# A graph kernel on one core: the node table stored twice, masked by mate, and 192 fetches of the search for 256

## The reference, cut to what matters

```python
h = (x_flat @ W_gat).reshape(M, HEADS, NUM_EXPERTS)      # 16 numbers a node
a_src = (h * att_src).sum(-1); a_dst = (h * att_dst).sum(-1)   # 4 scores each
e = leaky_relu(a_src[src] + a_dst[dst], 0.2)
alpha = softmax of e over the edges of one target node (a self loop is among them)
agg = segment_sum(h[src] * alpha[:, :, None], dst) + b_gat
scores = layernorm(agg).mean over heads; top 2 of 4 experts, softmax of the two
out = sum over experts of gate * (gelu(x @ W1[e] + b1[e]) @ W2[e] + b2[e])
```

## Time and profile before

| | us |
|---|---|
| median of 3 runs | 3634.56 |
| lowest and highest | 3616.6, 3640.06 |
| the profiled execution, its span | 3601.8 |
| front, up to the pause | 1773.6 |
| pause | 19.3 |
| edge loop, from its first turn | 1887 to 3601 |

### The profile page before, as it was taken

One profiled execution on the slowest core, in us unless ns is written; L12 is line 12 of the kernel. 1 busy time (PEld: TensorE's weight loads), 2 busy tenths in 40 slices (PEclk: granted clock), 3 DMA queues, 4 the chain that ended last, 5 costly groups with the idle time before them and its releaser, 6 DMA issues. The chain is left out here.

```text
span 3601.8 us, 31245 instructions
## 1 busy us (share of the span) xinstructions
PE 1935.1 (54%) x8829; PEld 1316.8 (37%) x8829; DVE 2257.8 (63%) x4422; ACT 1215.1 (34%) x2447; POOL 1857.5 (52%) x1723
## 2 busy tenths in 40 slices
PE   1776642387878645567432455454544444454555
PEld 1555542255655434456311222232222222222223
DVE  8999886989999965554223454454553444544547
ACT  2676754244444323455311122122212122121222
POOL 5400248554544444445575656655655656656561
PEclk9998865699999867777555676676776677767768
DMA  5792001011111121101111111111111111111111
GB/s 198 250 391 84 16 23 39 24 40 37 46 44 41 36 60 40 56 20 23 42 27 23 32 33 32 32 28 38 32 33 32 32 28 31 38 28 32 37 29 30
DMA packets 170130, 192.35 MB, mean 53 GB/s; under 512 B 59241, under 2 KB 126096, under 8 KB 169008
## 3 DMA queue, kind: packets, MB, share of 16 engines
q1 hardware_dynamic: 107616, 118.69, 9.9%
q0 software_dynamic: 57088, 62.48, 8.4%
q10 hardware_dynamic: 5328, 9.97, 0.7%
HBM read 91.70 MB, written 105.25 MB: 55 GB/s over the span
## 5 line engine op out<-in xcount | busy, mean ns | idle before, releaser
L1518 POOL DMA_INDIRECT edge_rows<-node_table,edge_ids x1024 | 1006.5, 983 | 646.2 <-POOLq L1243 345.9
L1646 PE MATMUL x_b_hid<-x_featT,x_w 128*128 128x512 f32 x512 | 362.3, 854 | 281.4 <-PEq L1243 93.5
L1146 POOL DMA_INDIRECT token_results<-arena,token_of x160 | 251.1, 1569 | 294.3 <-ACT arena L1082 216.9
L583 DVE TENSOR_TENSOR sort_ping<-sort_pong 128x1024 f32<-128x1024 f32 (+1 forms) x232 | 395.1, 1744 | 11.3 <-issue 3.8
L1158 POOL DMA_INDIRECT arena<-keys,row_ids x256 | 249.3, 974 | 288.6 <-DVE counts L821 181.0
L583 DVE TENSOR_TENSOR sort_pong<-sort_ping 128x1024 f32<-128x1024 f32 (+1 forms) x230 | 389.9, 1736 | 8.7 <-ACT sort_ping L1016 3.7
L1139 POOL DMA_INDIRECT slots<-arena,send x128 | 177.8, 1389 | 371.9 <-ACT arena L1038 336.9
L1640 PE MATMUL x_b_featT<-ident,x_feat 128*128 128x128 f32 x128 | 34.8, 428 | 581.0 <-issue 385.3
L1653 PEld LDWEIGHTS x_b_res<-x_w,x_hid 128*128 128x128 f32 x2048 | 276.1, 216 | 152.1 <-issue 152.1
L1653 PE MATMUL x_b_res<-x_w,x_hid 128*128 128x128 f32 x2048 | 303.9, 307 | 39.8 <-issue 39.8
L1646 PEld LDWEIGHTS x_b_hid<-x_featT,x_w 128*128 128x128 f32 x512 | 118.9, 262 | 500.2 <-issue 300.9
(11 more groups left out here) (346 smaller groups left out, 4059.0 us busy)
## 6 DMA issues: line engine op xcount, KB each, us to landing
edge_table<-zeros SPq DMA_DIRECT2D x8, 5120.0 KB, 35.7
edge_rows<-node_table,edge_ids POOLq DMA_INDIRECT x1024
arena<-slots SPq DMA_DIRECT2D x40, 260.0 KB
slots<-zeros SPq DMA_DIRECT2D x2, 5120.0 KB, 24.4
edge_table<-edge_rows SPq DMA_DIRECT2D x64, 160.0 KB
out_dram<-x_y ACTq DMA_DIRECT2D x33, 256.0 KB
x<-in_x_dram SPq DMA_DIRECT2D x4, 2048.0 KB, 20.2
adjacent<-in_adj_dram SPq DMA_DIRECT2D x32, 256.0 KB, 2.7
```

The source lines that it names most:

```text
L583: step(dve.tensor_tensor(vb[:, :, t, :], va[:, :, 0, :], va[:, :, 1, :], op))
L1146: pool.indirect_dma_start(rows_dram, bass.IndirectOffsetOnAxis(token_of[:, n % 4, r:r + 1], 0), res[:, n % 2, r, :], None, bounds_check=TO ...
L1518: pool.indirect_dma_start(rows[:, u, c, :], None, table_dram, bass.IndirectOffsetOnAxis(ids[:, u, c:c + 1], 0)).then_inc(rows_in[u], 16)
L1646: pe.matmul(b_hid[:, c % 2, :], w1[:, c // HC1, c % HC1 * P:(c % HC1 + 1) * P], featT[:, :], start=True, stop=True).then_inc(hid_mm, 1)
```

## The change

The 16 features of a node are stored twice. A row of `table_dram` now has 24 numbers: 16 features, four columns for mate 0's scores and four for mate 1's. The first 16,384 rows hold the source scores in mate 0's columns and -1e30 in mate 1's, the second 16,384 the other way round. The source index of an edge keeps its mate bit (mask `MATES * NODE_BIT - 1`), so an edge of mate 1 fetches its row from the second half, and its score for mate 0 is -1e30 by itself. DVE therefore needs to hide only what lies beyond the pair's last edge; and the search needn't know where mate 1 begins, so 64 of the 256 fetches (eight batches of 32) go. The projection has 52 columns (twice 24, and the four target scores) and adds the constant `apart`, which holds the -1e30. The tables in DRAM grow: `table_dram` to 32,768 x 24, `edges_dram` by 24 for 20 columns, cleared in twelve writes of at most 516 x 16 numbers a partition. `tab` is written by two DMAs a chunk. A window is 40 x 24 numbers.

```diff
-ROW = GAT + HEADS
-TAB = ROW + HEADS
+MATES = 2
+ROW = GAT + MATES * HEADS
+TAB = MATES * ROW + HEADS
...
-CLEAR = 640
+CLEAR, CLEAR_EDGES = 640, 516
...
     def dve(self, dve, n):
         dve.wait_ge(self.projected, n + 1)
-        dve.tensor_scalar(self.into[:, n * PER:(n + 1) * PER, :], self.b_out[n % 2][:, :, 0:self.cols], 1.0, None, ALU.mult).then_inc(self.kept, 1)
+        dve.tensor_tensor(self.into[:, n * PER:(n + 1) * PER, :], self.b_out[n % 2][:, :, 0:self.cols],
+                          self.offset.unsqueeze(1).to_broadcast([P, PER, self.cols]), ALU.add).then_inc(self.kept, 1)
...
-        gat_w, att, att_part = sb("gat_w", [P, TAB]), sb("att", [P, 2, GAT]), sb("att_part", [P, 2, GAT])
+        gat_w, apart, att, att_part = sb("gat_w", [P, TAB]), sb("apart", [P, TAB]), sb("att", [P, 2, GAT]), sb("att_part", [P, 2, GAT])
+        gat_row = gat_w[:, 0:MATES * ROW].rearrange("p (m c) -> p m c", m=MATES)
...
+        SEARCHED = [*range(0, GRAPHS, SEARCH), *range(GRAPHS + ALL_PAIRS, SEARCHES, SEARCH)]
...
             link(dve.memset(att0.right[:, :, :, 2 * FEAT:2 * FEAT + 1], 1.0))
-            dve.wait_ge(gat_in, 32)
+            link(dve.memset(apart[:, :], 0.0))
+            for m in range(MATES):
+                others = slice(m * ROW + GAT + (1 - m) * HEADS, m * ROW + GAT + (2 - m) * HEADS)
+                step(dve.memset(apart[:, others], -BIG))
+                step(dve.memset(gat_w[:, others], 0.0))
+            join()
+            dve.wait_ge(gat_in, 48)
             dve.tensor_tensor(att_part[:, :, :], att[:, :, :], gat_w[:, 0:GAT].unsqueeze(1).to_broadcast([P, 2, GAT]), ALU.mult).then_inc(gat_made, 1)
             dve.wait_ge(gat_made, 1)
-            dve.tensor_reduce(gat_w[:, GAT:TAB], att_part[:, :, :].rearrange("p a (h e) -> p (a h) e", h=HEADS), AX_X, ALU.add).then_inc(gat_made, 1)
+            for side, at in ((0, GAT), (1, MATES * ROW)):
+                dve.tensor_reduce(gat_w[:, at:at + HEADS], att_part[:, side, :].rearrange("p (h e) -> p h e", h=HEADS), AX_X, ALU.add).then_inc(gat_made, 1)
+            dve.wait_ge(gat_made, 3)
+            dve.tensor_copy(gat_row[:, 1, GAT + HEADS:ROW], gat_row[:, 0, GAT:GAT + HEADS]).then_inc(gat_made, 1)
...
-                cols = slice(n * SEARCH, (n + 1) * SEARCH)
+                cols = slice(SEARCHED[n], SEARCHED[n] + SEARCH)
...
-                    link(dve.tensor_scalar(tiles_u, table[:, :].bitcast(U32), NODE_BIT - 1, None, ALU.bitwise_and))
+                    link(dve.tensor_scalar(tiles_u, table[:, :].bitcast(U32), MATES * NODE_BIT - 1, None, ALU.bitwise_and))
...
-                if n >= 0 and n % 4 != 3:
+                if n >= 0 and n % 4 != 3 and searched[0] < len(SEARCHED):
...
-            dve.scalar_tensor_tensor(found[:, 0, :], rows_f, float(FAN), counts[:, :], ALU.mult, ALU.add)
+            for cols in (slice(0, GRAPHS), slice(GRAPHS + ALL_PAIRS, SEARCHES)):
+                dve.scalar_tensor_tensor(found[:, 0, cols], rows_f[:, cols], float(FAN), counts[:, cols], ALU.mult, ALU.add)
...
-            sp.dma_start(gat_w[:, 0:GAT], a["gat_w"]).then_inc(gat_in, 16)
+            for m in range(MATES):
+                sp.dma_start(gat_row[:, m, 0:GAT], a["gat_w"]).then_inc(gat_in, 16)
...
-            clear(sp, edges_dram, cleared)
+            clear(sp, edges_dram, cleared, CLEAR_EDGES)
...
-            table_v = table_dram.rearrange("(b i) c -> i b c", i=NODES)
+            sp.wait_ge(cleared, clears(edges_dram, CLEAR_EDGES) * 16 + 16)
+            table_v = table_dram.rearrange("(m b i) c -> m i b c", m=MATES, i=NODES)
             for c in range(GROUPS // CHUNK):
                 cols = slice(c * CHUNK * PER, (c + 1) * CHUNK * PER)
                 sp.wait_ge(gat.kept, (c + 1) * CHUNK)
-                sp.dma_start(table_v[:, cols, :], tab[:, cols, :]).then_inc(tabled, 16)
-            sp.wait_ge(tabled, 16 * (GROUPS // CHUNK))
+                for m in range(MATES):
+                    sp.dma_start(table_v[m][:, cols, :], tab[:, cols, m * ROW:(m + 1) * ROW]).then_inc(tabled, 16)
+            sp.wait_ge(tabled, 16 * MATES * (GROUPS // CHUNK))
...
-            for n in range(SEARCHES // SEARCH):
+            for n in range(len(SEARCHED)):
                 ge(pool, looked, n - FETCHED + 1)
                 for c in range(SEARCH):
-                    q = n * SEARCH + c
+                    q = SEARCHED[n] + c
...
-            link(dve.tensor_tensor(by_mate(left[:, 0:GRAPHS], 0), by_unit(second_of[:, 0:ALL_PAIRS]), by_unit(first_edge), ALU.subtract))
-            link(dve.tensor_copy(by_mate(left[:, 0:GRAPHS], 1), by_unit(pair_degree[:, :])))
+            link(dve.tensor_copy(left[:, 0:ALL_PAIRS], pair_degree[:, :]))
...
-                last_mates, theirs = bass.ds(theirs * UNIT + PAIRS, PAIRS), bass.ds(theirs * UNIT, UNIT)
+                theirs = bass.ds(theirs * PAIRS, PAIRS)
...
-                    step(dve.tensor_tensor(sc[:, m * PAIRS:(m + 1) * PAIRS, :, :], w[:, :, :, GAT:ROW],
-                                           node[:, mates[m], ROW:TAB].unsqueeze(2).to_broadcast(HALF_FULL), ALU.add))
-                step(dve.tensor_tensor(hide[:, :, :], order[:, :].unsqueeze(1).to_broadcast([P, UNIT, WINDOW]),
-                                       left[:, theirs].unsqueeze(2).to_broadcast([P, UNIT, WINDOW]), ALU.is_ge))
+                    step(dve.tensor_tensor(sc[:, m * PAIRS:(m + 1) * PAIRS, :, :], w[:, :, :, GAT + m * HEADS:GAT + (m + 1) * HEADS],
+                                           node[:, mates[m], MATES * ROW:TAB].unsqueeze(2).to_broadcast(HALF_FULL), ALU.add))
+                step(dve.tensor_tensor(hide[:, :, :], order[:, :].unsqueeze(1).to_broadcast([P, PAIRS, WINDOW]),
+                                       left[:, theirs].unsqueeze(2).to_broadcast([P, PAIRS, WINDOW]), ALU.is_ge))
                 settle()
                 step(dve.scalar_tensor_tensor(flat, flat, SLOPE, flat, ALU.mult, ALU.max))
-                step(dve.scalar_tensor_tensor(hide[:, PAIRS:UNIT, :], hide[:, PAIRS:UNIT, :], 1.0, hide[:, 0:PAIRS, :], ALU.add, ALU.subtract))
+                step(dve.tensor_scalar(hide[:, :, :], hide[:, :, :], -BIG, None, ALU.mult))
                 step(dve.tensor_scalar(left[:, theirs], left[:, theirs], -float(WINDOW), None, ALU.add))
                 settle()
-                step(dve.scalar_tensor_tensor(sc[:, :, :, :], hide[:, :, :].unsqueeze(3).to_broadcast(FULL), -BIG, sc[:, :, :, :], ALU.mult, ALU.add))
-                step(dve.tensor_scalar(adv[:, :], left[:, last_mates], 0.0, float(WINDOW), ALU.is_gt, ALU.mult))
+                step(dve.tensor_tensor(by_pair, by_pair, hide[:, :, :].rearrange("p t k -> p (t k)").unsqueeze(1).unsqueeze(3).to_broadcast([P, MATES, PAIRS * WINDOW, HEADS]), ALU.add))
+                step(dve.tensor_scalar(adv[:, :], left[:, pair], 0.0, float(WINDOW), ALU.is_gt, ALU.mult))
```

More of the change, by code:

```diff
@@ L54 @@
 UNITS = GRAPHS // UNIT
-MATES = 2
 PAIRS = UNIT // MATES
@@ L353, with __init__ @@
 class Projection:
-    def __init__(self, sem, tag, x, rstd, shift, ident, weight, cols, into, view, banks, lo=0, turned_in=(0, 1), put_in=(2, 3)):
+    def __init__(self, sem, tag, x, rstd, shift, ident, weight, offset, cols, into, view, banks, lo=0, turned_in=(0, 1), put_in=(2, 3)):
         self.feat, self.featT = view(lo, 2, PER, FEAT), view(lo + 1024, 2, PER, NODES)
@@ L359, in __init__ @@
             sem(f"{tag}_{n}") for n in ("normed", "turned", "featT", "projected", "kept"))
-        self.x, self.rstd, self.shift, self.ident, self.weight, self.cols, self.into = x, rstd, shift, ident, weight, cols, into
+        self.x, self.rstd, self.shift, self.ident, self.weight, self.offset, self.cols, self.into = x, rstd, shift, ident, weight, offset, cols, into
     def act_step(self, act, n, u):
@@ L471, in front @@
         LAG, CHUNK = 12, GROUPS // 4
-        gat = Projection(sem, "gat", x, rstd, shift, ident, gat_w[:, :], TAB, tab, view, banks, 4112, (1, 1), (3, 3))
+        gat = Projection(sem, "gat", x, rstd, shift, ident, gat_w[:, 0:TAB], apart[:, :], TAB, tab, view, banks, 4112, (1, 1), (3, 3))
         gat_norms = []
@@ L544, in front, with clears, clear @@
                      (spread_a, NODE_BIT << 16), (spread_b, 3 * NODE_BIT << LOG_NODES))
-        def clears(table):
-            return -(-(math.prod(table.shape) // P) // (CLEAR * REPEAT))
-        def clear(sp, table, done):
+        def clears(table, widest=CLEAR):
+            return -(-(math.prod(table.shape) // P) // (widest * REPEAT))
+        def clear(sp, table, done, widest=CLEAR):
             flat = table.rearrange("(p r) d -> p (r d)", p=P)
-            width = math.gcd(flat.shape[1], CLEAR)
-            for c in range(clears(table)):
-                part = flat[:, c * CLEAR * REPEAT:min((c + 1) * CLEAR * REPEAT, flat.shape[1])].rearrange("p (r w) -> p r w", w=width)
+            width = math.gcd(flat.shape[1], widest)
+            for c in range(clears(table, widest)):
```

(5 more changed lines are left out.)

22 lines of the change are left out of this document (11 added, 11 removed).

## The result

The changed kernel took 3652.47 us in the median of 17 runs (3630.34 to 3673.64), the kernel before 3634.56 (3616.6 to 3651.02, 17 runs): ratio 1.0047, interval [1.0027, 1.0068]. I had forecast 3613 with a range of 3565 to 3645. Measured again later with both kernels as they are, the ratio was 1.0120 [1.0080, 1.0159], against 1.000 [0.9978, 1.0022] for a second copy of the kernel before. So the change costs 0.5 to 1.2%, and the first thing to explain is why 21 us that should have gone came back as a loss of 18 to 47.

What follows compares the result with a forecast made beforehand. Bound: POOL's chain of 34 indirect DMAs per edge-loop turn. Front -17 - 8 + 3 + 0.5 + 1 = -20.5, loop +4 - 5 = -1, together -21.5 us: 3613, range 3565 to 3645.

Steps and rivals of the forecast that it cites:

- The fetches and searches: Search's tail: steps without fetch bursts save 10.5 and 6.5 us, together 17; bounds 0 and 24.
- the projection: 52 columns for 24 and a longer DVE instruction: +3 us in the search loop, +0.5 in the tail.
- Rival 1: Search's tail: the bursts don't stall it, so the 17 us saving is 0 and the time 3630; chance 0.22.
- The pause: Between last projection and edge loop: 15.4 us shrink to the table's write alone, taken as 7.5; save 8.
- The clearing: Clearing writes grow from nine to twelve, some 20 us, covered before POOL's first send: 0; without that cover 20.
- The edge write: Head of each turn: 196 KB for 164 inside POOL's 2.7 us wait, 0.15 us x 29 = +4.
- The masks: DVE's masks in each turn: dense part 0.13 us shorter, worth nothing by itself in all turns but the last three.
- two or three more turns: Edge loop: stall onset shifted by 0.28 us, so two or three turns change class, 2 to 4 us each: -5.
- the sign of being wrong: Edge loop: the forecast is wrong if the mean turn moves by more than 0.5 us either way.
- Rival 3: Gap ahead of first L1480: larger rows bring stalls earlier, more turns lengthen by 4.3 us; 3682 with 16; chance 0.08.
- Rival 2: Edge loop: twelve of fifteen long turns get through L1468 in time, 49 us more saved: 3564; chance 0.15.
- The port: New mask tensor_scalar could lock GpSimd out, 7 us, forecast 3620; rejected, as POOL's gathers begin later.

Runs made afterwards that it cites:

- search192: The kernel before with only the 192 fetches for 256 and 24 searches, the bounds between the mates read from other columns: ratio 0.9893.
- rows24: The kernel before with only the wider rows, 24 numbers for 20, table stored once, old masks, all 256 fetches: ratio 1.0062.
- masks: The kernel before with only the new mask instructions on the old table, first mate not masked: ratio 1.0118, repeated at 1.0152.
- pool_late: The kernel before with two semaphore increments on POOL ahead of its burst of gathers, DVE unchanged: ratio 1.0136.
- before_again: The kernel before, unchanged, measured and profiled a second time: ratio 1.000, mean turn 56.11 us.
- after_again: The changed kernel, unchanged, measured again on the same chip as the kernel before: ratio 1.0120, mean turn 59.34 us.
- masks_slow: The kernel before with the new mask instructions alone plus one extra 80-element compare in every turn: ratio 1.000.
- pace_early: The changed kernel with POOL waiting behind its windows for an earlier DVE point, the multiply by the inverse root: ratio 1.0104 to the kernel before.
- pace: The changed kernel with POOL waiting behind its two windows until DVE reaches its wait for the experts' matmul: ratio 0.9595 to the kernel before.

## Why the prediction was wrong, step by step

- **The fetches and searches, -17**, the projection, +3.5: together -13.5 forecast for the time to the last projection, -19.3 measured in the first pair of profiles. The tail without fetches runs at 3.33 us a step; more of the bursts' cost went than the stop I could point at. If the projection costs its 3.5, the fetches gave 22.8 in this pair, just inside the upper bound of 24; no run has the projection alone. Rival 1 is out: search192, with the fetches and their searches gone and nothing else, gains 39 us.
- **The pause, -8**: 19.3 to 10.9, -8.4. SP waits 5.3 us for the table in place of 4.7, near the 5 that I had worked out for two writes that share the engines and far from the 10 of two in a row; 7.5 was too careful. L389 takes 0.374 us, as worked out (0.373).
- **The clearing, 0**: the first send starts at 378.4 for 375.7, and ACT ends its wait in both kernels; in the second profile of the kernel before, with the small clearing, it starts at 379.1, so the 2.7 us are spread. The first turn opens 24 to 28 us earlier in the two pairs, more than the forecast 20.5. No cost of the clearing shows.
- **The edge write, +4**: POOL starts 0.11 us later (0.15 taken). By length that is 3 us, as said. But it is nearly half of the 0.24 us by which the distance shrinks: rows24, which has it without the masks, loses 0.6%, 22 us.
- **The masks, "worth nothing by itself"**: this is the step that failed. The size was right (0.12 us, 0.13 forecast). I then reasoned that DVE 0.13 us earlier and POOL 0.15 us later would let two or three more turns get through L1468 ahead of the stalls, -5 us. Both shifts have the other sign: by masks and pool_late, each of them makes turns longer. In place of -1 us for the loop, the second pair of profiles shows +90 (mean turn 56.1 to 59.3), and the first result, 18 us of loss over a front some 28 us shorter, about +46. I had in effect taken the onset of the stalls as fixed on POOL's clock. It isn't: DVE's first idle gap of more than 0.9 us behind the long reduction (L1426) begins, in the median, 24.0 us into the turn in before_again and at 22.4 in masks and after_again and 22.5 in pool_late, some 1.6 us earlier for shifts of 0.12 to 0.24 (in the first two profiles only 24.2 and 23.7). An engine that comes early to a place where others contend isn't thereby past it. I had looked at one place, the onset 23 us into the turn, and had counted turns of 51 and 55 us there; the distance that goes with the loss lies 2.7 us into it, where POOL's first gather meets DVE's masks. And the mean turn moved by more than the 0.5 us that I had named as the sign of being wrong.
- **Rival 3** named what happened, the gap ahead of the first L1480, its price (4.3 us a turn; measured 59.3 to 59.4 against 55.2 to 55.6 for an ordinary one) and its threshold. I gave it 0.08, since "as many DMAs go out as before, on the same pitch". Its cause was only partly right: it blamed the larger rows and windows, which alone make 12 long turns and 22 us; the shorter masks, which it didn't have, do more. One turn of 31 did it already, which I should have read as a state that the kernel can fall into in every turn, not as a rare mishap. By the sum of rival 3, 28 long turns in place of 4 are 24 x 4.3 = 103 us; 90 were measured. (Rival 2 at its full size, 3564, lay 1 us outside the range that I said took it in.)
- **The port.** I weighed a rule of the Trainium skill ("SBUF — State Buffer", section "Who interferes with whom"): a DVE tensor_scalar can lock GpSimd out of writing descriptors. It would have cost 7 us by the new instruction's own length, and I said that POOL hasn't begun by then. The traces bear that out: it runs from 1.82 to 2.02 us of the turn in masks, and POOL's first gather starts at 2.69 there as in the kernel before. (masks_slow has it in every turn at 1.000 [0.9972, 1.0028], but that interval is 10 us wide on either side and couldn't show 7.) But the first gather does seem to wait for DVE: its length, 1.22 to 0.97 us, follows the start of the reduction, behind the 640-element instruction and the small tensor_scalar that precede it. This fits the rule; no run changed those two alone, so it isn't shown which of the two instructions holds the gather.

What stays open: how a first gather that is held up 0.25 us less turns into a stop of 11 us forty microseconds later, and why the same kernel at the same distance had 12 long turns in one profile and 28 in another. The earlier onset isn't the whole way from the one to the other, since it doesn't sort the turns: in rows24, 3 of the 11 turns with an onset before 22.6 us are long, and 9 of the 17 with a later one. From the second gather on, the distance of POOL to DVE is the same in all kernels of the table, 1.01 to 1.02 us behind the reduction's start; so what differs is what lies ahead of it, the edge write and the first gather against all the rest.

## What to carry to other kernels

In a loop whose turns fall into classes, count the classes before pricing an edit, and take every shift of tenths between two engines as a risk in both directions, faster work included. Where one engine issues a long burst of indirect DMAs and the others stand still in it, try a wait that places the burst: here it gave 3.3% on the kernel before, against 1.1% for the fetches and the searches, and one placed a few microseconds too early gave nothing (pace_early, 1.0104). And profile the kernel before more than once: its span was 33 us below its own median, and of the 73 us by which the first two profiles differ in the loop nearly half was that.

## What the runs showed of the hardware

- In the later part of a long burst of indirect DMAs, DVE takes one step with a wait per 1.3 to 1.4 us (after_again, L1481 to L1483, idle 1.08 to 1.24 ahead of each), near the gathers' pitch of 1.25; ACT's L1607 comes 1.8 to 2.8 us apart there. At times DVE, ACT and PE all stop, for 11 to 12 us, and go on some 6.5 us behind the start of the last DMA (2702.66, 2709.13). In pace DVE's slow steps end near 2365, 4 us behind the end of the last DMA.
- An indirect DMA of 128 rows keeps POOL busy for 0.95 us and is followed by 0.30 us of issue, with rows of 80 and 96 bytes and for windows of 3,200 and 3,840 bytes alike (medians 0.94 to 0.95 in the profiles of both kernels).
- One DVE instruction of 0.235 us at the head of a turn and not at its end made a kernel of 3.7 ms 1.2% faster (1.0119 to 1.0002), and two semaphore increments on POOL, 0.16 us, made another 1.4% slower.
